# Attention probabilities through device memory: four block writes and one read in place of one write and four block reads

## The chip, the cores and the metric

One core of one Trainium2 chip runs the whole kernel in one launch. The metric is the device time of the execution in microseconds (us). A core has five engines that run side by side: TensorE (PE: matmuls; its weight loads are the row PEld), VectorE (DVE), ScalarE (ACT), GpSimd (POOL) and SyncE (SP), which here issues all transfers. Sixteen DMA engines move the bytes between device memory and the on-chip memory of 128 partitions.

## The reference

Two layers over 8 batches of 112 rows and 1024 columns, with 375 context rows per batch. Each layer adds a cross attention and then a small mixture of low-rank experts. The part that matters here is the second layer's attention, with 32 query heads over 8 key and value heads of width 128:

```python
q = (query @ wq).reshape(bs, sq, HQ, DK).transpose(0, 2, 1, 3)
k = (key @ wk).reshape(bs, sk, HKV, DK)
v = (value @ wv).reshape(bs, sk, HKV, DV)
...
q = apply_rope(q, pos)
k = apply_rope(k, curr_seq_pos + jnp.arange(sk))
scores = jnp.einsum('bhqd,bhkd->bhqk', q, k) / scale
...
attn = jax.nn.softmax(scores + m[:, None, :, :], axis=-1)
out = jnp.einsum('bhqk,bhkd->bhqd', attn, v)
out = out.transpose(0, 2, 1, 3).reshape(bs, sq, HQ * DV)
return out @ wo
```

## The kernel before, in words

Every large product is made of three float32r passes, from a high and a low part of each operand (`split_product`, L200): ScalarE makes the high part, GpSimd or VectorE the low one.

The second layer's attention runs in 64 steps, one for each of 8 groups (a key and value head with its four query heads) and 8 batches. All 64 steps are unrolled, in `attention_phase`. In step s TensorE makes the scores of step s+3, then adds a part of the output projection for an earlier quad of batches (`project`, two tiles of 448 columns, which needs weights of `wo`), then the product of probabilities and values of step s. VectorE masks scores, normalises and turns the probabilities of step s+2 and makes low parts; ScalarE takes the exponentials and makes high parts. ScalarE ends a step with `split_wo`, which waits for the next pieces of `wo` (names `e_raw_wo` and `e_wo_*`, L1902), and begins the next one with `take_output` (L1907), the high part of the last head output (`e_o_t_*`), whose low part VectorE then makes (L1977). `project` needs both parts.

For that product the probabilities must lie with the keys on the partitions. VectorE's transpose works within squares of 32 by 32 (L1739). The 112 queries are laid out as 4 blocks of 28 in a field of 4 blocks of 32 rows, and so the transpose leaves each key block j in the partitions of query block i. The blocks then have to change places, from (i; j) to (j; i), and this is done through device memory: `carry_out` writes the turned tile (`in_blocks`, shown as `q_rotated_then_x_rows`) to the internal tensor `probabilities`, and `carry_in` reads it back into `pt_raw` (two buffers, shown as `e_shuffled` and `e_shuffled_then_xn_t`). A tile is 128 partitions by 1536 float32, 768 KB.

SyncE carries out its instructions in order, one list for all transfers. In a step it does: `carry_out` of step s+2 (waits for the transpose), `load_qk` of step s+6, `load_v` of step s+2, `carry_in` of step s+2 (waits until the write has landed), then one or two pieces of `wo` (256 KB each; none in some steps). The order is written out by hand. All these transfers go through the same queue.

Of the kernel before, what the change touches and what calls it, by code (L numbers as in the profile page):

```python
# [12 lines left out]
F32 = mybir.dt.float32  # L13
# [5 lines left out]
P = 128  # L19
BATCH, SEQ, DIM = 8, 112, 1024  # L20
KEYS = 375
KEYS_EVEN = 376
KEY_TILES = 3
# [5 lines left out]
GROUPS, PER_GROUP = 8, 4  # L29
# [176 lines left out]
def build(nc, x, ctx_nat, ctx_t, mask, wq0_t, wk0, bq, bk, a0, b0, wq1, wk1, wv1, wo1, a1, b1,  # L206
          rope_q, rope_k, ident_in, tri0_in, order1_in, out):
    kt_dram = nc.dram_tensor("k_rotated", (BATCH, GROUPS, P, KEYS_EVEN), F32, kind="Internal").ap()
    v_dram = nc.dram_tensor("v_rows", (GROUPS, BATCH, P, KEY_TILES, P), F32, kind="Internal").ap()
    q_dram = nc.dram_tensor("q_rotated", (HEADS // 2, BATCH, P, 2, SEQ), F32, kind="Internal").ap()  # L210
    p_dram = nc.dram_tensor("probabilities", (2, P, BLOCKS, PER_GROUP * KEY_TILES * BLOCK), F32, kind="Internal").ap()
    x2_dram = nc.dram_tensor("x_after_layer0", (BATCH, SEQ, DIM), F32, kind="Internal").ap()
    with ExitStack() as outer:
        def sb(name, shape, dt=F32, ctx=outer):
            return ctx.enter_context(nc.sbuf_tensor(name, shape, dt))

        def sem(name, ctx=outer):
            return ctx.enter_context(nc.semaphore(name))

        banks = [outer.enter_context(nc.psum_tensor(f"bank{i}", [P, 512], F32)) for i in range(8)]  # L220
        k = Shared()
        k.x, k.ctx_nat, k.ctx_t, k.mask, k.ident_in, k.out = x, ctx_nat, ctx_t, mask, ident_in, out
        k.wq0_t, k.wk0, k.bq, k.bk = wq0_t, wk0, bq, bk
        k.wq1, k.wk1, k.wv1, k.wo1 = wq1, wk1, wv1, wo1
        k.a0, k.b0, k.a1, k.b1, k.tri0, k.order1 = a0, b0, a1, b1, tri0_in, order1_in
        k.rope_q, k.rope_k = rope_q, rope_k
        k.kt_dram, k.v_dram, k.q_dram, k.x2_dram, k.p_dram = kt_dram, v_dram, q_dram, x2_dram, p_dram
        k.banks, k.passed, k.sem = banks, sem("passed"), sem

        k.tables = sem("tables_in")  # L230
        k.ident, k.minus_half = sb("ident", [P, P]), sb("minus_half", [SEQ, 1])
        with ExitStack() as heads, ExitStack() as layer0:

            k.qp = sb("qp_then_xn3", [P, CH, TOK], ctx=layer0)
            k.qb = sb("q_dot_bk", [SEQ, BATCH], ctx=layer0)
            share_operands(nc, k, layer0)
            query_phase(nc, k)
            with ExitStack() as context, nc.Block() as block:

                keep, keep_pair, _ = buffers_of(nc, context)  # L240
                k.w_rest = keep_pair("w_rest", [P, CH - 2, DIM])
                keys, chunks = KeySems(sem), ContextSems(sem)
                k.layer0_only, k.k_stored = context, keys.stored
                q1 = QuerySems(sem)
                key_phase(nc, k, keys, chunks, block)
                layer0_phase(nc, k, keys, chunks, q1, heads, block)
                context.close()
                first = AttentionSteps(nc, heads, k)
                rotation = rotation_buffers(nc, layer0)
                layer0.close()  # L250
                late = attention_buffers(nc, heads, k, first)
                last_heads = query1_phase(nc, k, first, q1, rotation, block)
                attention_phase(nc, k, first, late, last_heads, heads, block)
# [1332 lines left out]
class AttentionSteps:  # L1586
# [140 lines left out]
    def transpose(self, dve, s, u, heads):  # L1727


        t, h = u % 2, heads[0]  # L1730
        if h == 0:
            dve.wait_ge(self.normed, 2 * s + 2)
            if s >= 2:
                dve.wait_ge(self.shuffled[t], 64 * (s // 2))
        else:
            dve.wait_ge(self.last_normed, 2 * s + 2)
        take_waits(dve, self.k.passed)
        piece = KEY_TILES * BLOCK
        dve.transpose(self.in_blocks[:, t, :, h * piece:(h + 2) * piece].rearrange("p j (m k) -> p m j k", k=BLOCK),  # L1739
                      self.s_buf[:, t, h:h + 2, :].rearrange("p h (c j k) -> p (h c) j k", j=BLOCKS, k=BLOCK)  # L1740
                      ).then_inc(self.transposed, 1)

    def carry_out(self, sp, s):


        t = s % 2
        sp.wait_ge(self.transposed, 2 * s + 2)
        if s >= 2:
            sp.wait_ge(self.shuffled[t], 64 * (s // 2))
        sp.dma_start(self.k.p_dram[t], self.in_blocks[:, t]).then_inc(self.carried, 16)  # L1750

    def carry_in(self, sp, s):


        t = s % 2
        sp.wait_ge(self.carried, 16 * s + 16)
        if s >= 2:
            sp.wait_ge(self.pt_low_first, s - 1)
            sp.wait_ge(self.pt_low, 2 * s - 2)
        for j in range(BLOCKS):  # L1760
            sp.dma_start(self.pt_raw[t][BLOCK * j:BLOCK * (j + 1)],  # L1761
                         self.k.p_dram[t, :, j].rearrange("(i a) x -> a i x", i=BLOCKS)).then_inc(
                self.shuffled[t], 16)

    def load_mask(self, sp):
        sp.dma_start(self.mask, self.k.mask).then_inc(self.mask_in, 16)
# [49 lines left out]
def attention_phase(nc, k, first, late, last_heads, ctx, block):  # L1816
# [79 lines left out]
    @block.scalar  # L1896
    def _(act):
        def split_wo(g, n):
            act.wait_ge(wo_in[n % 2], 16 * (4 * g + n // 2) + 16)
            if g > 0:  # L1900
                act.wait_ge(y_acc, 16 * g + n - 7)
            act.activation(wo_half(0, n), raw_wo[:, n % 2, 0], ACT.Copy).then_inc(wo_high, 1)  # L1902

        def take_output(s):
            u = s % BATCH
            act.wait_ge(o_acc, s + 1)
            act.activation(o_columns(ot[0][u // 4], u), by_block(o_banks[s % 2][:, 0:HALF]),  # L1907
                           ACT.Copy).then_inc(o_high, 1)

        def step(s, u, g):  # L1910
            if s >= 1:
                take_output(s - 1)
            if 0 < s < STEPS - 2:
                first.normalise_last(act, s + 2, u)
            act.wait_ge(first.shuffled[s % 2], 64 * (s // 2) + 64)
            for c in range(KEY_TILES):
                act.activation(by_block(pt[0][:, c, :]), raw_p(s, c), ACT.Copy).then_inc(pt_high, 1)  # L1917
            if s == 0:
                first.normalise_last(act, 2, u)
            if s + AHEAD < STEPS:  # L1920
                first.exps(act, s + AHEAD, u + AHEAD, (0, 1))
            if s + 5 < STEPS:
                first.qk_high_part(act, s + 5, u + 5)
            if s + AHEAD < STEPS:
                first.exps(act, s + AHEAD, u + AHEAD, (2, 3))
            if s + 1 < STEPS:
                first.v_high_part(act, s + 1, u + 1)
            for n in wo_splits(u, g):
                split_wo(g, n)

        steps(act, step)
        take_output(STEPS - 1)

# [197 lines left out]
def final_phase(nc, k, first, sem, block, y_added, y_of_quad):  # L2131
# [39 lines left out]
    @block.sync  # L2171
    def _(sp):
        sp.wait_ge(first.masked, 4 * GROUPS * BATCH)
        sp.wait_ge(first.qk_low, 2 * GROUPS * BATCH)
        sp.dma_start(aw[:, :, :], k.a1).then_inc(consts, 16)
        sp.dma_start(order, k.order1).then_inc(consts, 16)
        sp.dma_start(bw[:, :], k.b1).then_inc(consts, 16)

        def load(b):
            if b >= SLOTS:  # L2180
                sp.wait_ge(moved[b % SLOTS], 32 * (b // SLOTS))
            sp.dma_start(xr[:, b % SLOTS], k.x2_dram[b]).then_inc(moved[b % SLOTS], 16)

        for b in range(SLOTS):
            if b == 2:
                for s in first.shuffled:
                    sp.wait_ge(s, 64 * GROUPS * BATCH // 2)
            load(b)
        for b in range(LAST):
            sp.wait_ge(sl.added, 2 * b + 2)  # L2190
            sp.dma_start(k.out[b], xr[:, b % SLOTS]).then_inc(moved[b % SLOTS], 16)
            if b + SLOTS < BATCH:
                load(b + SLOTS)
        for h in range(2):
            cols = slice(h * 512, (h + 1) * 512)
            sp.wait_ge(sl.added, 2 * LAST + h + 1)
            sp.dma_start(k.out[LAST, :, cols], xr[:, LAST % SLOTS, cols]).then_inc(moved[LAST % SLOTS], 16)
        for i, s in enumerate(moved):
            sp.wait_ge(s, 32 * len(range(i, BATCH, SLOTS)) + (16 if i == LAST % SLOTS else 0))
# [232 lines left out]
```

## Time and profile before

| | |
|---|---|
| median of 3 runs | 1772.06 us (1770.04 to 1773.93) |
| profiled execution | 1774.46 us, of which the span from first to last instruction is 1772.7 us |
| TensorE, share of the span busy | 98% |
| VectorE, ScalarE, GpSimd | 62%, 41%, 44% |
| memory read and written | 193.01 MB and 97.26 MB, 164 GB/s over the span |
| write of a tile, and one of its four reads, from issue to landing | 4.7 us and 3.9 us in the median |

The profile shows one execution. Shares are of the whole span, which has stages with different limits; the attention of the second layer takes the part from about 1085 us to 1700 us. A row `SPq` is an instruction of SyncE's queue, where the time is that of issuing the transfer, and a row `DMA` is the transfer in flight.

### The profile page before, as it was taken

The page shows a single profiled execution, that of the slowest core. Times are in us where ns is not written, and L with a number is a line of the kernel's source. Part 1 is how long each engine was busy: PE and PEld are TensorE (multiplying, and loading weights), DVE is VectorE, ACT ScalarE, POOL GpSimd, SP SyncE. Part 2 cuts the span into 40 slices and gives each one's busy share as a digit, 9 for nine tenths or more (in the row PEclk, how much of TensorE's full clock was granted, in tenths as well). Part 3 has the DMA queues.
Part 4 walks back from the last instruction along what each step waited for, and adds up shares of the span by engine and source line. Part 5 has one row for each costly group of instructions (what it writes and reads, how often), then busy time and mean ns, then how long its engine had stood idle before and what let it go on. Part 6 is the DMA issues. An engine that isn't in the chain of part 4 may idle for free.

```text
span 1772.7 us, 26431 instructions
## 1 busy us (share of the span) xinstructions
PE 1736.4 (98%) x8904; PEld 1579.1 (89%) x8904; DVE 1101.1 (62%) x2116; ACT 733.5 (41%) x1532; POOL 782.3 (44%) x588
## 2 busy tenths in 40 slices
PE   6999999999999999999999999999999999999998
PEld 6999999999888888888999999889999899999986
DVE  7631276566433333336666668898888888888845
ACT  5211210012333232222101014477887888888724
POOL 3223522125422222201222234487787877877634
PEclk9999999999999999999999999999999999999999
DMA  4212442235643333423433335699999999999833
GB/s 140 63 49 83 133 133 84 85 104 162 208 128 119 111 116 118 128 82 95 129 109 91 106 113 163 200 291 272 274 277 274 270 275 281 276 272 281 257 117 111
DMA packets 186403, 291.55 MB, mean 164 GB/s; under 512 B 48337, under 2 KB 146897, under 8 KB 185281
## 3 DMA queue, kind: packets, MB, share of 16 engines
q1 hardware_dynamic: 186304, 290.33, 55.7%
q8 instruction: 51, 0.84, 0.2%
q14 instruction: 48, 0.39, 0.1%
HBM read 193.01 MB, written 97.26 MB: 164 GB/s over the span
## 4 chain that ended last, share of the span: by engine, by line
PE 70%; DMA 8%; DVE 5%; POOL 2%; issue 2%; ACT 2%; SPq 1%; DVEq 0%; ACTq 0%; POOLq 0%
PE bank L200 65%; DMA probabilities<-q_rotated_then_x_rows 3%; DMA e_raw_wo<-in_wo 3%; SPq L1761 1%; DVE e_scores L1696 1%; POOL shared_operand_low L324 1%; PE bank L106 1%; DVE q_rotated_then_x_rows L1739 1%; PE bank L2317 1%; DVE e_p_t_low L1982 1%; PE bank L186 1%; PE bank L2330 1%; DMA aw_weights_then_ctx_rows<-in_wv 1%; DMA aw_weights_then_ctx_rows<-in_wk 0%; DMA ctx_raw<-in_ctx_t 0%
## 5 line engine op out<-in xcount | busy, mean ns | idle before, releaser
L200 PE MATMUL bank<-shared_operand_high,w_first_high 128*128 128x448 f32 (+1 forms) x768 | 279.1, 363 | 1.9 <-DVE shared_operand_low L558 1.2
L200 PE MATMUL bank<-shared_operand_high,w_first_low 128*128 128x448 f32 (+1 forms) x768 | 278.4, 362 | 0.0
L200 PE MATMUL bank<-shared_operand_low,w_first_high 128*128 128x448 f32 (+1 forms) x768 | 278.3, 362 | 0.0
L324 POOL TENSOR_TENSOR shared_operand_low<-ctx_raw,shared_operand_high 128x768 fp32r<-128x768 f32 x64 | 119.2, 1875 | 199.6 <-ACT shared_operand_high L320 199.4
L1704 ACT ACTIVATE e_scores<-e_scores,e_least 128x375 f32<-128x375 f32 x256 | 153.5, 601 | 44.9 <-DVE e_least L1696 44.9
L1452 POOL TENSOR_TENSOR w_first_low<-aw_weights_then_ctx_rows,w_first_high 128x1024 fp32r<-128x1024 f32 x30 | 72.2, 2407 | 221.1 <-ACT w_first_high L1420 221.1
L200 PEld LDWEIGHTS bank<-shared_operand_high,w_first_high 128*128 128x128 f32 x768 | 144.7, 188 | 13.1 <-POOL w_first_low L496 1.4
L200 PEld LDWEIGHTS bank<-shared_operand_low,w_first_high 128*128 128x128 f32 x768 | 144.8, 189 | 11.0
L200 PEld LDWEIGHTS bank<-shared_operand_high,w_first_low 128*128 128x128 f32 x768 | 144.6, 188 | 11.0
L320 ACT ACTIVATE shared_operand_high<-ctx_raw 128x768 fp32r<-128x768 f32 x64 | 52.8, 843 | 211.8 <-DMA ctx_raw<-in_ctx_t 193.2
L1696 DVE CUSTOM_DVE_ANT_0 e_scores<-bank,e_mask_then_layer_ffn 128x375 f32<-128x375 f32 x256 | 134.8, 529 | 0.0
L1420 ACT ACTIVATE w_first_high<-aw_weights_then_ctx_rows 128x1024 fp32r<-128x1024 f32 x30 | 31.8, 1060 | 236.7 <-PE bank L200 194.8
L200 PE MATMUL bank<-shared_operand_high,w_rest_high 128*128 128x376 f32 x384 | 128.7, 335 | 0.2 <-POOL w_rest_low L789 0.2
L200 PE MATMUL bank<-shared_operand_high,w_rest_low 128*128 128x376 f32 x384 | 128.6, 335 | 0.0
L200 PE MATMUL bank<-shared_operand_low,w_rest_high 128*128 128x376 f32 x384 | 128.6, 335 | 0.0
L1739 DVE STREAM_TRANSPOSE q_rotated_then_x_rows<-e_scores 128x768 f32<-128x768 f32 x128 | 124.1, 970 | 0.3 <-DVE e_scores L1717 0.3
L200 PE MATMUL bank<-w_rest_high,shared_operand_high 128*128 128x512 f32 x288 | 112.9, 392 | 0.0
L200 PE MATMUL bank<-w_rest_high,shared_operand_low 128*128 128x512 f32 x288 | 112.4, 390 | 0.0
L200 PE MATMUL bank<-w_rest_low,shared_operand_high 128*128 128x512 f32 x288 | 112.3, 390 | 0.0
L1939 POOL TENSOR_TENSOR e_p_t_low<-e_shuffled_then_xn_t,e_p_t_high 128x448 fp32r<-128x448 f32 x64 | 84.0, 1333 | 40.7 <-ACT e_p_t_high L1917 40.6
L1939 POOL TENSOR_TENSOR e_p_t_low<-e_shuffled,e_p_t_high 128x448 fp32r<-128x448 f32 x64 | 83.9, 1332 | 35.6 <-ACT e_p_t_high L1917 35.5
L1025 ACT ACTIVATE v_out<-bank 128x512 f32<-128x512 f32 x48 | 28.6, 596 | 171.3 <-PE bank L200 171.3
(259 smaller groups left out, 4614.7 us busy)
## 6 DMA issues: line engine op xcount, KB each, us to landing
probabilities<-q_rotated_then_x_rows SPq DMA_DIRECT2D x64, 768.0 KB, 4.7
ctx_raw<-in_ctx_t SPq DMA_DIRECT2D x64, 384.0 KB, 3.9
e_shuffled_then_xn_t<-probabilities SPq DMA_DIRECT2D x128, 192.0 KB, 3.9
e_shuffled<-probabilities SPq DMA_DIRECT2D x128, 192.0 KB, 3.9
e_raw_wo<-in_wo SPq DMA_DIRECT2D x64, 256.0 KB, 4.8
aw_weights_then_ctx_rows<-in_wq SPq DMA_DIRECT2D x30, 512.0 KB, 4.0
q_rotated<-q_rotated_then_x_rows SPq DMA_DIRECT2D x64, 224.0 KB, 2.3
e_raw_then_a<-q_rotated SPq DMA_DIRECT2D x64, 224.0 KB, 5.0
```

Source lines behind the costliest of these rows:

```text
L106: last = pe.transpose(banks[j][:, c * SEQ:(c + 1) * SEQ], buf.xn[:, k, ch * P:(ch + 1) * P], ident[0:SEQ, 0:SEQ])
L186: last = pe.matmul(mid[:, 0:width], xnt[:, c, :], aw[:, c, :], start=(c == 0), stop=(c == CH - 1))
L200: mm = pe.matmul(out, stationary[a], moving[b], start=(first and i == 0), stop=(last and i == 2))
L320: act.activation(k.ctx_ring[0][slot][:, 2 * j:2 * j + 2, :], k.c_raw[:, j % 2], ACT.Copy).then_inc(done, 1)
L324: pool.tensor_tensor(k.ctx_ring[1][slot][:, 2 * j:2 * j + 2, :], k.c_raw[:, j % 2], f32(k.ctx_ring[0][slot][:, 2 * j:2 * j + 2, :]), ALU.s ...
L1025: act.activation(v_out[:, p % 2], v_bank[p % 2][:, :], ACT.Copy).then_inc(v_read, 1)
L1420: act.activation(k.w_first[0][:, t], k.raw[:, t], ACT.Copy).then_inc(w_high, 1)
L1452: pool.tensor_tensor(k.w_first[1][:, t], k.raw[:, t], f32(k.w_first[0][:, t]), ALU.subtract).then_inc(w_low, 1)
L1696: dve.tensor_tensor_reduce(self.s_buf[:, t, h, 0:KEYS], self.s_bank[h][:, 0:KEYS], self.mask[:, u, :], 1.0, HIGHEST, ALU.add, ALU.min, sel ...
L1704: act.activation(self.s_buf[:, t, h, 0:KEYS], self.s_buf[:, t, h, 0:KEYS], ACT.Exp, bias=self.least[:, t, h:h + 1], scale=-1.0, accum_out= ...
L1739: dve.transpose(self.in_blocks[:, t, :, h * piece:(h + 2) * piece].rearrange("p j (m k) -> p m j k", k=BLOCK), self.s_buf[:, t, h:h + 2, : ...
L1939: pool.tensor_tensor(by_block(pt[1][:, c, :]), raw_p(s, c), by_block(f32(pt[0][:, c, :])), ALU.subtract).then_inc(pt_low, 1)
```

## The change

The internal tensor is laid out by destination instead of by source: its second index is the key block j, the third the row within the block, the fourth the query block i. The write is now four transfers, one for each query block i, each from 32 partitions with four pieces of 1536 bytes to where they belong. The read is one transfer of 128 rows of 6144 bytes. The counts that others wait for follow: a write now adds 64 to its semaphore, a read 16. Lines behind the functions move up by one.

```diff
-    p_dram = nc.dram_tensor("probabilities", (2, P, BLOCKS, PER_GROUP * KEY_TILES * BLOCK), F32, kind="Internal").ap()
+    p_dram = nc.dram_tensor("probabilities", (2, BLOCKS, BLOCK, BLOCKS, PER_GROUP * KEY_TILES * BLOCK), F32, kind="Internal").ap()
...
-                dve.wait_ge(self.shuffled[t], 64 * (s // 2))
+                dve.wait_ge(self.shuffled[t], 16 * (s // 2))
...
         if s >= 2:
-            sp.wait_ge(self.shuffled[t], 64 * (s // 2))
-        sp.dma_start(self.k.p_dram[t], self.in_blocks[:, t]).then_inc(self.carried, 16)
+            sp.wait_ge(self.shuffled[t], 16 * (s // 2))
+        for i in range(BLOCKS):
+            sp.dma_start(self.k.p_dram[t, :, :, i].rearrange("j a x -> a j x"),
+                         self.in_blocks[BLOCK * i:BLOCK * (i + 1), t]).then_inc(self.carried, 16)
...
-        sp.wait_ge(self.carried, 16 * s + 16)
+        sp.wait_ge(self.carried, 64 * s + 64)
...
-        for j in range(BLOCKS):
-            sp.dma_start(self.pt_raw[t][BLOCK * j:BLOCK * (j + 1)],
-                         self.k.p_dram[t, :, j].rearrange("(i a) x -> a i x", i=BLOCKS)).then_inc(
-                self.shuffled[t], 16)
+        sp.dma_start(self.pt_raw[t], self.k.p_dram[t].rearrange("j a i x -> (j a) i x")).then_inc(self.shuffled[t], 16)
...
-            act.wait_ge(first.shuffled[s % 2], 64 * (s // 2) + 64)
+            act.wait_ge(first.shuffled[s % 2], 16 * (s // 2) + 16)
```

On SyncE, in the kernel before, the first steps of the attention stand like this (a row with x4 is four transfers, one after the other):

```order
L1750 DMA probabilities<-q_rotated_then_x_rows 128x1536
L1632 DMA e_raw_then_a<-q_rotated 128x2x224
L1634 DMA e_raw_then_a<-k_rotated 128x376
L1639 DMA e_raw_then_a<-v_rows 128x384
L1761 DMA e_shuffled_then_xn_t<-probabilities 32x4x384 x4
L1875 DMA e_raw_wo<-in_wo 128x512
```

The changed kernel has the same place with the four in front:

```order
L1751 DMA probabilities<-q_rotated_then_x_rows 32x4x384 x4
L1632 DMA e_raw_then_a<-q_rotated 128x2x224
L1634 DMA e_raw_then_a<-k_rotated 128x376
L1639 DMA e_raw_then_a<-v_rows 128x384
L1762 DMA e_shuffled_then_xn_t<-probabilities 128x1536
L1874 DMA e_raw_wo<-in_wo 128x512
```

The loads of q, k and v now stand behind four transfers instead of one, and the load of `wo` behind one instead of four; nothing changes its place otherwise.

## Rows read from the trace of the kernel before

**Rows 1.** The page's busy row, and busy time by stage with its columns
```profile
PE 1736.4 (98%) x8904; PEld 1579.1 (89%) x8904; DVE 1101.1 (62%) x2116; ACT 733.5 (41%) x1532; POOL 782.3 (44%) x588
...
core 0: us, PE busy (x) PEld busy (x) DVE busy (x) ACT busy (x) POOL busy (x), PEclk, DMA share, GB/s
...
1240.00:1684.00 444.00, 439.06 (x2234) 411.24 (x2234) 377.27 (x840) 358.20 (x886) 345.37 (x295) 1.00 0.95 274
```

**Rows 2.** TensorE's waits, 1240 to 1700 us: total us, times, longest
```profile
PE bank L200 <- DVE e_o_t_first_low L1977: 4.9, 5, 2.0
PE bank L200 <- DVE e_o_t_second_low L1977: 2.2, 1, 2.2
```

**Rows 3.** The chain that ended last, 1369 to 1384 us: start, us, what
```profile
1369.65 5.15 DMA probabilities<-q_rotated_then_x_rows
...
1374.81 0.33 SPq L1761
...
1376.13 0.43 SPq L1761
...
1377.08 5.13 DMA e_raw_wo<-in_wo
...
1382.23 0.63 ACT e_wo_third_high L1902
1382.86 0.44 ACT e_o_t_first_high L1907
...
1383.33 0.64 DVE e_o_t_first_low L1977
```

**Rows 4.** Busy time by stretch behind two stalls, columns as in rows 1
```profile
1384.00:1388.00 4.00, 4.00 (x12) 3.58 (x13) 4.00 (x10) 4.00 (x11) 3.52 (x4) 0.57 0.88 215
1388.00:1392.00 4.00, 4.00 (x22) 3.70 (x21) 2.39 (x7) 2.09 (x6) 3.36 (x4) 1.00 1.04 314
1694.00:1698.00 4.00, 3.71 (x11) 3.36 (x12) 1.20 (x2) 0.67 (x2) 2.68 (x3) 0.60 1.04 309
```

**Rows 5.** The whole chain that ended last, share of the span by line
```profile
by line: PE bank L200 65.5%; DMA probabilities<-q_rotated_then_x_rows 3.2%; DMA e_raw_wo<-in_wo 2.7%; issue 1.9%; SPq L1761 1.1%; DVE e_scores L1696 1.0%; POOL shared_operand_low L324 0.9%; PE bank L106 0.8%; DVE q_rotated_then_x_rows L1739
```

**Rows 6.** All 64 writes, L1750: issue in ns, first and last; landing
```profile
L1750 SPq DMA_DIRECT2D probabilities<-q_rotated_then_x_rows x64: 326/338/504, 1087.9 to 1681.2; - x64
...
DMA to landing us min/median/max: 3.8/4.7/6.7
```

**Rows 7.** SyncE's queue in the last step: start, us of issue, what
```profile
1685.96 1.74 SPq L1761 DMA_DIRECT2D e_shuffled<-probabilities  x4
1687.75 0.43 SPq L1875 DMA_DIRECT2D e_raw_wo<-in_wo  x1
```

**Rows 8.** SyncE's own waits before the reads: total us, times, longest
```profile
SPq L1761 <- DMA probabilities<-q_rotated_then_x_rows: 131.4, 64, 4.0
```

**Rows 9.** Landing of the four reads issued from 1685.96 us
```profile
DMA to landing us min/median/max: 3.0/3.8/4.3
```

**Rows 10.** Transfers by line: count, KB each, median us from issue to landing
```profile
k_rotated<-k_rotated_sb SPq DMA_DIRECT2D x64, 188.0 KB, 1.9
...
aw_weights_then_ctx_rows<-in_ctx_nat SPq DMA_DIRECT2D x7, 1536.0 KB, 6.6
aw_weights_then_ctx_rows<-in_wk SPq DMA_DIRECT2D x16, 512.0 KB, 3.6
```

**Rows 11.** ScalarE's timeline: the wait for wo behind those last reads
```profile
1692.21 0.63 ACT L1902 ACTIVATE e_wo_fourth_high<-e_raw_wo 128x512 fp32r<-128x512 f32 x1 [5.27 <-DMA e_raw_wo<-in_wo]
```

**Rows 12.** 448 KB over 112 partitions: seven stores, L2191, and three loads, L2182
```profile
DMA to landing us min/median/max: 3.1/3.1/3.5
...
DMA to landing us min/median/max: 3.4/3.5/3.5
```

**Rows 13.** Two stores of 224 KB, L1354, issued one behind the other
```profile
L1354 SPq DMA_DIRECT2D q_rotated<-q_rotated_then_x_rows x2: 434/474/513, 1118.1 to 1118.6; - x2
...
DMA to landing us min/median/max: 6.1/6.2/6.3
```

More of the change, by code:

```diff
@@ L2186, in _ @@
                 for s in first.shuffled:
-                    sp.wait_ge(s, 64 * GROUPS * BATCH // 2)
+                    sp.wait_ge(s, 16 * GROUPS * BATCH // 2)
             load(b)
```

## The prediction

> **What bounds the kernel now.** I read the stages first [rows 1]. TensorE is busy for 1736 of 1773 us. In the long middle stage (1240 to 1684) TensorE is busy for 439.1 of 444 us, and the 16 DMA engines for 0.95 of the time: both are nearly full, at full clock. The transfers that change lie behind 1087 us; the change can gain only what TensorE loses from there on.
>
> That loss is in the waits of the matmuls [rows 2]: 4.9 us in five waits and 2.2 us in one, together 7.1 us, all for a split head output (DVE, L1977). The chain shows why that comes late [rows 3]: last transpose of the probabilities, the write of them (5.15 us), four issues of reads on SyncE's queue, two loads of wo (the second in flight 5.13 us), the split of that weight on ScalarE, and only behind it ScalarE's copy of the head output, then DVE's, then TensorE, which had been idle for 2 us. ScalarE stands in line for wo, and wo stands in SyncE's queue behind the probabilities. The kernel pays for a stall a second time: after the one at 1384 us and the one at 1694 us the granted clock is 0.57 and 0.60 over the next 4 us, a mean between the levels of 1.2 and 2.4 GHz, against 1.00 afterwards; 12 matmuls run in 4 us where 22 do then, so that each stall costs some 1.6 us more [rows 4].
>
> How often does this chain set the end? Of the whole chain, 3.2% are these writes, 2.7% loads of wo and 1.1% issues of the four reads [rows 5]. 1.1% of 1772.7 is 19.5 us; a set of four takes 1.75 us (from 1374.81 to the end of the one of 1376.13, [rows 3]), so 11 passes of the 64.
>
> **The change, part by part.** Per step it removes one write of 128 rows and four reads of 32 partitions, and adds four writes of 32 partitions and one read of 128 rows. Bytes, number of transfers and waits of other engines stay.
>
> *Issue on SyncE.* One plain write costs 0.34 us [rows 6], four reads 1.74 [rows 7]. The other way about, the four writes take about 1.8 and the read 0.34. The write side gets 1.4 us longer, and the loads of q, k and v behind it leave 1.4 us later. They have cover: SyncE afterwards waits for the write, 131.4 us in 64 times, 2.05 us a step [rows 8], and these loads are for steps 6 and 2 ahead. Without that cover a late v would hold ScalarE by the same 1.4 us. The read side gets 1.4 us shorter, and wo leaves that much earlier.
>
> *The read.* The last four reads show what pieces cost. The first lands 3.0 us after its issue, the last 4.3 us after its own [rows 9], which begins 1.3 us after the first (1374.81 and 1376.13 in [rows 3]), so the set needs 5.6 us. Three pieces in 5.6 - 3.0 = 2.6 us is 0.87 us for 192 KB. A whole read of 768 KB isn't in the trace. From loads over all 128 partitions, 512 KB in 3.6 and 1536 KB in 6.6 [rows 10], 768 KB interpolate to 3.6 + 3.0/4 = 4.35, say 4.4 us. So here the read would land 1.2 us sooner than the set. Bounds: nothing, if memory and not the pieces sets the pace, and 1.9 us (5.6 less the 3.8 of the fastest whole write, [rows 6], rounded up). I take 1.2, near the interpolated value.
>
> Does wo's earlier issue bring anything by itself? In the last step wo is issued at 1687.75 [rows 7], 0.5 after the fourth read (1687.3), which lands at 1691.6 with its 4.3 us. ScalarE begins on wo at 1692.21 [rows 11], so wo lands no more than 0.6 us behind the reads. It flows behind the reads' data in the same queues, so it lands when they have drained, not 1.4 us sooner. I count 0.1 for it.
>
> *The write.* A whole write lands in 3.8 at best, 4.7 in the median, 6.7 at worst [rows 6]. Written in pieces of 32 partitions: one small store over 128 partitions lands in 1.9 (188 KB) [rows 10]; a piece of 32 partitions needs 0.3 more if stores suffer as loads do (0.87 us for 192 KB in pieces, 0.56 at the 3.0 us for 1024 KB of the whole loads), then three more at 0.87 to 1.0 each: 1.9 + 0.3 + 2.8 = 5.0 us on free queues, against 3.8 for the whole one at best [rows 6]. That is 1.2 us later. Do stores suffer like loads? The nearest rows: a store of 448 KB over 112 partitions lands in 3.1 us and the load of the same shape in 3.4 to 3.5 [rows 12], so one shape costs nearly the same in both directions. Bounds: nothing (then the writes are done when the last, issued 1.4 us late, lands 1.9 later, 3.3 us, inside the present 4.7), and 1.9 us, the mirror of the read's.
>
> The Trainium skill (SBUF — State Buffer, Door 1: The DMA port swizzle) says that 32 partitions reach 8 of the 16 ports, with 189 GB/s measured at 1 MiB against 328 for all 128. By that estimate 768 KB would take 1.8 us longer in pieces, so the write would lose 1.8 and the read win 1.8, and the sum would be the same. The trace's pieces, 0.87 us for 192 KB, are 226 GB/s, nearer to the rule's slow figure than to its fast one. The same skill (DMA: Bandwidth & Descriptors, Rules for kernel authors) advises one transfer over 128 partitions in place of several over parts; it speaks against the write's half of the change and for the read's.
>
> *The sum.* Per pass: read -1.2, wo -0.1, write +1.2: -0.1 us. Over 11 passes about -1 us, which lies within the 7.1 us of waits that could be saved. The profiled execution took 1774.46 us, 1772.70 of them span, so it would take 1773.4; it lies 2.4 us above the median of 1772.06. From the median: **1771.0 us**.
>
> **The rivals.**
> *A: stores don't suffer.* TensorE would gain 1.2 or 1.3 us a pass. The stalls are at most 2.2 us long and a stall often follows on two passes, so most of the 7.1 us go and with them up to 3.2 us of low clock: 6 to 10 us, 1762 to 1766, say 1764.5. For it speaks that small stores over 128 partitions land in 1.9 us; against it the like times of load and store in [rows 12]. Chance 0.25.
> *B: the write gets longer by more than the read gets shorter.* The place is SyncE's wait before the read. It decides as soon as the last of the four writes lands more than 1.3 us later than the whole write does (6.0 in the median). At the bound of 1.9 a pass costs 0.6 us, 11 passes 6.6 us, and 5 to 8 us if a stall more or less falls to the low clock: 1778.5. For it: the DMA engines are at 0.95, so nothing absorbs a longer transfer, and where pieces of two kinds overlap (a slow read of wo behind, writes ahead) both may slow. Against: the read's gain has the same cause as the write's loss. Chance 0.22.
> *C: each write waits for its predecessor to be confirmed in memory.* The trace has two stores of 224 KB issued 0.5 us apart, which land 6.1 and 6.3 us after their issues, that is 0.7 us apart [rows 13]: back to back. With a full small-store latency of 1.9 each, the four would take 7.6, 2.9 later than now, or 1.6 a pass after the gain of 1.3: 11 times 1.6 is 18 us, 1790. Chance 0.03.
> The Trainium skill (DMA: Bandwidth & Descriptors, Anatomy of one DMA) states that the semaphore fires only when the last byte is confirmed, slowest when memory is the target; this is the only reading under which C would follow, and the two stores speak against it.
>
> **How the numbers follow.** Within 0.2% (3.5 us) is about what a measurement here can tell from no change. The forecast, read and write cancel to within 0.4 us a pass, has 0.50 and its own range is 1768 to 1775. A 0.25, B 0.22, C 0.03. The range takes in the middle of A and of B: 1764.5 to 1778.5; beyond it lie C, the far half of A and part of B, 2 in 10. Faster by over 0.2%: A and a little of the forecast, 0.29. Slower: B, C and a sliver, 0.26. Same: 0.45.
>
> **What the changed profile would show.** The issues on SyncE's queue: four writes with about 0.45 us each, one read with 0.34. Landing of the writes: the last should land 5.5 to 6.2 us after the first one's issue (rival A: 4.7 or less, B: over 6.2). Landing of the read: 4.2 to 4.8 (median), against 5.6 to 6 for the set before. Landing of the pair: 10.4 to 10.8 us after the last transpose in both kernels. The waits of TensorE for L1977 should stay between 5 and 8 us, and at most two stretches with a low clock. Share of the DMA engines 0.93 to 0.97 in the middle stage. My prediction is wrong if the whole read lands no sooner than the set did, or if the loads of k and v, pushed back by 1.4 us, start to hold ScalarE: a row of waits for e_v_high or e_k_high beyond 2 us would show it.

## The result, and the profile after

The changed kernel takes 1797.88 us in the median of 4 runs (1794.87 to 1801.64), the kernel before 1772.74 us in the median of 4 runs of the same session. The ratio is 1.0146 with a 95% interval from 1.0129 to 1.0164: slower by 25 us, where 1771.0 was predicted and 1778.5 was the upper end of the range. That is 1.5%, and the interval lies clear of 1. The profiled execution of the changed kernel took 1798.12 us.

The page's busy row and the middle stage of the changed kernel, with the columns of [rows 1]:

```profile
PE 1747.0 (97%) x8904; PEld 1583.3 (88%) x8904; DVE 1103.5 (61%) x2116; ACT 733.3 (41%) x1532; POOL 783.1 (44%) x588
...
1240.00:1684.00 444.00, 426.62 (x2144) 395.50 (x2143) 365.02 (x811) 345.75 (x859) 336.26 (x287) 0.99 0.87 265
```

TensorE does the same 8904 matmuls in 10.6 us more busy time (1747.0 against 1736.4), and outside them the span has 49.3 us instead of 36.3 (1796.3 - 1747.0 and 1772.7 - 1736.4). These two, 10.6 and 13.0, are the whole difference of the spans, 23.6 us. The 13.0 are idle time. Of the 10.6 only a part is the price of the clock. Spans and mean granted clock, first of the kernel before, then of the changed one:

```profile
core 0: 1772.7 us, clock 0.997
core 0: 1796.3 us, clock 0.995
```

A share of 0.003 of 1772.7 us is 5 us of full-speed work that is missing, 0.005 of 1796.3 us is 9, so the clock explains some 4 of the 10.6 us. Another 2.2 stand ahead of 1080 us, where both kernels are alike (1064.0 us busy in the one trace, 1066.3 in the other). What the last 4 us are was not taken apart. Four microseconds at a time (same columns; the third from the end is the granted clock) the trace shows how they hang together:

```profile
1392.00:1396.00 4.00, 1.56 (x9) 1.24 (x8) 0.27 (x2) 1.77 (x4) 1.14 (x2) 1.00 0.99 337
1396.00:1400.00 4.00, 3.37 (x11) 3.05 (x12) 4.00 (x11) 4.00 (x11) 3.46 (x4) 0.70 0.68 222
1400.00:1404.00 4.00, 4.00 (x19) 3.65 (x19) 2.54 (x8) 2.60 (x7) 4.00 (x5) 0.87 0.78 215
1404.00:1408.00 4.00, 4.00 (x23) 3.85 (x22) 3.30 (x9) 2.82 (x6) 1.15 (x2) 1.00 0.93 255
```

TensorE stands idle for 2.4 of 4 us, and in the next two stretches, at a granted clock of 0.70 and 0.87, it does 11 and 19 matmuls where 23 go at full clock, as in [rows 4]. The DMA engines are less busy than before, 0.87 against 0.95: the change relieves them and still loses time. (Over the same stretch the share is 0.84 in the kernel below with the single read alone and 0.95 in the one with the four writes alone, so the relief is the single read's.)

TensorE's waits from 1240 to 1700 us (total us, times, longest), to be read beside [rows 2]:

```profile
PE bank L200 <- DVE e_o_t_first_low L1976: 9.8, 7, 3.1
PE bank L200 <- DVE e_p_t_low L1981: 7.2, 5, 2.3
PE bank L200 <- DVE e_o_t_second_low L1976: 0.6, 1, 0.6
```

Together 17.6 us instead of 7.1, and with a second kind: the low part of the next probabilities (L1981) is late too, because VectorE itself is: in this stretch it waits 64.6 us for ScalarE's high parts of the output, where it waited 57.3 in the kernel before. The whole chain by line, to be read beside [rows 5]:

```profile
by line: PE bank L200 53.1%; DMA e_raw_wo<-in_wo 7.4%; DMA probabilities<-q_rotated_then_x_rows 5.2%; issue 3.6%; DVE e_scores L1696 2.2%; DVE q_rotated_then_x_rows L1739 1.8%; DVE e_p_t_low L1981 1.6%; SPq L1751 1.4%; DVE e_scores L1717 1.
```

Counted piece by piece from 1080 us on, the chain passes over a load of wo 21 times, and 10 times in the kernel before, in 64 steps. The stretch of the chain that corresponds to [rows 3] (start, us, what):

```profile
1368.78 6.69 DMA e_raw_wo<-in_wo
...
1375.49 0.63 ACT e_wo_first_high L1901
1376.12 0.44 ACT e_o_t_first_high L1906
...
1376.59 0.07 DVE e_o_t_first_low L1976
...
1379.28 0.93 DVE e_p_t_low L1981
...
1380.67 0.90 DVE q_rotated_then_x_rows L1739
...
1381.59 0.33 SPq L1751
...
1382.92 3.79 DMA probabilities<-q_rotated_then_x_rows
...
1386.73 0.33 SPq L1762
...
1387.58 7.26 DMA e_raw_wo<-in_wo
...
1395.95 0.64 DVE e_o_t_first_low L1976
1396.63 9.55 PE bank L200 x39
```

This is the row that the prediction had not looked for. Between 1375.49 and 1381.59 the chain does not go through TensorE at all: from the landing of wo it goes over ScalarE and VectorE to the next transpose, and from there into the next write. It closes into a loop: transpose, write, read, wo, ScalarE, VectorE, transpose. One turn takes two steps: these loads of wo follow the read of one step, and the transpose that they hold back belongs to the step after the next. The part from the landing of wo to the next write is 6.1 us (1375.47 to 1381.59), the part from the write's first issue to the landing of wo 13.25 us (1381.59 to 1394.84).

The transfers by line on the page (KB each, median us from issue to landing; before, the write took 4.7 and one of the four reads 3.9):

```profile
probabilities<-q_rotated_then_x_rows SPq DMA_DIRECT2D x256, 192.0 KB, 3.6
...
e_shuffled_then_xn_t<-probabilities SPq DMA_DIRECT2D x32, 768.0 KB, 5.5
e_shuffled<-probabilities SPq DMA_DIRECT2D x32, 768.0 KB, 5.7
e_raw_wo<-in_wo SPq DMA_DIRECT2D x64, 256.0 KB, 5.8
```

The single read takes 5.5 to 5.7 us, where 4.2 to 4.8 was predicted. SyncE's queue shows what stands ahead of it. First one step of the kernel before, then one of the changed kernel (start, us of issue, what):

```profile
1369.65 0.34 SPq L1750 DMA_DIRECT2D probabilities<-q_rotated_then_x_rows  x1
1370.03 0.43 SPq L1632 DMA_DIRECT2D e_raw_then_a<-q_rotated  x1
1370.51 0.97 SPq L1634 DMA_DIRECT2D e_raw_then_a<-k_rotated  x1
1371.52 1.19 SPq L1639 DMA_DIRECT2D e_raw_then_a<-v_rows  x1
1374.81 1.75 SPq L1761 DMA_DIRECT2D e_shuffled_then_xn_t<-probabilities  x4
```

```profile
1381.59 2.29 SPq L1751 DMA_DIRECT2D probabilities<-q_rotated_then_x_rows  x4
1383.93 0.79 SPq L1632 DMA_DIRECT2D e_raw_then_a<-q_rotated  x1
1384.76 0.92 SPq L1634 DMA_DIRECT2D e_raw_then_a<-k_rotated  x1
1385.73 0.45 SPq L1639 DMA_DIRECT2D e_raw_then_a<-v_rows  x1
1386.73 0.33 SPq L1762 DMA_DIRECT2D e_shuffled_then_xn_t<-probabilities  x1
```

Before, the issue of v ends 2.1 us ahead of the reads (1372.71 and 1374.81); now 0.55 us ahead of the read (1386.18 and 1386.73), so that more of their data is still to come. Over the steps 13 to 60 v lands 1.6 us after the reads' first issue in the kernel before and 2.5 us after the read's issue in the changed one (medians).

### The profile page after: what moved, and what is told of

Same layout as the page of the kernel before. It is cut to its first block, busy times and chain, and to the rows that moved or that the text cites. A ratio compares the mean times of both kernels' runs of the same rounds, so it can differ in the third digit from the quotient of the medians.

```text
span 1796.3 us, 26431 instructions
## 1 busy us (share of the span) xinstructions
PE 1747.0 (97%) x8904; PEld 1583.3 (88%) x8904; DVE 1103.5 (61%) x2116; ACT 733.3 (41%) x1532; POOL 783.1 (44%) x588
## 4 chain that ended last, share of the span: by engine, by line
PE 57%; DMA 14%; DVE 9%; issue 4%; ACT 2%; SPq 2%; POOL 1%; DVEq 0%; ACTq 0%; POOLq 0%
PE bank L200 53%; DMA e_raw_wo<-in_wo 7%; DMA probabilities<-q_rotated_then_x_rows 5%; DVE e_scores L1696 2%; DVE q_rotated_then_x_rows L1739 2%; DVE e_p_t_low L1981 2%; SPq L1751 1%; DVE e_scores L1717 1%; PE bank L106 1%; PE bank L2316 1%; PE bank L186 1%; PE bank L2329 1%; POOL shared_operand_low L324 1%; DMA aw_weights_then_ctx_rows<-in_wk 0%; DVE y_t L1970 0%
## 5 line engine op out<-in xcount | busy, mean ns | idle before, releaser
L1717 DVE TENSOR_SCALAR e_scores<-e_scores,e_inv 128x375 f32<-128x375 f32 x128 | 99.0, 775 | 2.2
```

What stands on the lines that cost most here:

```text
L1717: dve.tensor_scalar(self.s_buf[:, t, h, 0:KEYS], self.s_buf[:, t, h, 0:KEYS], self.inv[:, t, h:h + 1], None, ALU.mult).then_inc(self.norme ...
```

## The experiments

The main readings of all kernels stand in one table. For each of the steps 13 to 60 the trace gives the end of the last transpose (T), the issue of each transfer and its landing; the figures are medians over these 48 steps, in us. "Write" and "read" are from the first issue of the set to its last landing, "T to T" is from one T to the next. Wo is loaded in 42 of these 48 steps; in the two kernels with a dash it is not behind the read. The time is the median, the ratio is to the kernel before in the same session, with its 95% interval.

| kernel | write | read | T to reads landed | T to wo landed | T to T | time, ratio |
|---|---|---|---|---|---|---|
| before | 4.72 | 6.01 | 10.98 | 11.61 | 8.76 | 1772.74 |
| changed | 5.42 | 5.81 | 11.62 | 12.40 | 9.23 | 1797.88, 1.0146 |
| w4_r4 | 5.70 | 6.30 | 12.16 | 12.94 | 9.33 | 1805.27, 1.0182 (1.0165 to 1.0199) |
| w1_r1_noswap | 4.06 | 4.34 | 8.48 | 9.50 | 8.76 | 1763.54, 0.9952 (0.9936 to 0.9969) |
| w4rows_r4 | 5.53 | 6.36 | 12.04 | 12.83 | 9.43 | 1807.28, 1.0201 (1.0184 to 1.0218) |
| w4spread_r1 | 5.20 | 5.35 | 10.83 | 11.69 | 8.79 | 1783.98, 1.0061 (1.0045 to 1.0077) |
| w1short_r4 | 4.80 | 5.96 | 11.07 | 11.74 | 8.86 | 1774.47, 1.0016 (1.0001 to 1.0030) |
| before_qkv_first | 6.39 | 5.79 | 13.99 | 14.86 | 10.46 | 1858.14, 1.0503 (1.0482 to 1.0524) |
| after_qkv_first | 7.68 | 4.35 | 13.26 | 14.52 | 10.14 | 1844.03, 1.0403 (1.0381 to 1.0426) |
| before_qkv_last | 4.70 | 5.95 | 10.58 | 11.38 | 10.35 | 1859.34, 1.0490 (1.0465 to 1.0514) |
| after_qkv_last | 5.46 | 4.32 | 9.93 | 11.02 | 9.98 | 1858.28, 1.0478 (1.0460 to 1.0497) |
| before_wo_first | 4.23 | 6.31 | 10.96 | - | 8.76 | 1763.09, 0.9955 (0.9939 to 0.9972) |
| after_wo_first | 5.75 | 6.36 | 12.22 | - | 8.76 | 1765.51, 0.9955 (0.9937 to 0.9972) |

**The write half alone.** Four writes, and four reads, whose rows now lie whole in device memory (6144 bytes, where they were gathered from pieces of 1536):

```diff
-        sp.dma_start(self.k.p_dram[t], self.in_blocks[:, t]).then_inc(self.carried, 16)
+        for i in range(BLOCKS):
+            sp.dma_start(self.k.p_dram[t, :, :, i].rearrange("j a x -> a j x"),
+                         self.in_blocks[BLOCK * i:BLOCK * (i + 1), t]).then_inc(self.carried, 16)
...
+            sp.dma_start(self.pt_raw[t][BLOCK * j:BLOCK * (j + 1)], self.k.p_dram[t, j]).then_inc(self.shuffled[t], 16)
```

> The write's half of the change alone: four scattered writes from 32 partitions each, and four reads into 32 partitions each. Before takes 1772.7, the changed kernel 1797.9. If the loss lies in the writes and in the loads of q, k and v that they push back, and the whole read gives something back, this is the slowest: 1803 to 1815, writes landing 5.4 in the median (4.7 before), set of reads 6.0 to 6.7. Rival, the loss lies in the whole read (it stands undivided behind other loads): 1772 to 1780 here.

It is 1.82% slower, 32 us, and so worse than the whole change. The writes land 1.0 us later, and T to wo grows by 1.3 us. The four reads gain nothing from their whole rows (6.30 against 6.01), so it is not the run length that makes a single read quicker.

**The read half alone.** One write, one read, the exchange left out:

```diff
-        for j in range(BLOCKS):
-            sp.dma_start(self.pt_raw[t][BLOCK * j:BLOCK * (j + 1)],
-                         self.k.p_dram[t, :, j].rearrange("(i a) x -> a i x", i=BLOCKS)).then_inc(
-                self.shuffled[t], 16)
+        sp.dma_start(self.pt_raw[t], self.k.p_dram[t]).then_inc(self.shuffled[t], 16)
```

> The read's half alone: one write and one read of 128 rows each; the exchange of the blocks is left out, so the probabilities reach the product in the wrong places. If the whole read is as quick as the best rows say (4.4 us free), it lands 4.8 to 5.2 in the median against 6.0 for the set before, and the kernel takes 1762 to 1768. Rival, a whole read brings nothing in this stream of transfers: lands 5.6 or more, time within 2 us of 1772.7.

Here the read lands 1.7 us sooner (4.34 against 6.01), more than the 1.2 of the prediction, and T to wo falls by 2.1 us. V lands 1.6 us after the read's issue, as before, so the loads ahead of it have the same lead. The write, which is the one of before, lands 0.7 us sooner too (4.06 against 4.72). The time falls by only 9 us. TensorE's waits from 1240 to 1700 us and the busy time of that stretch say why there is no more to win:

```profile
PE bank L200 <- DVE e_o_t_second_low L1974: 0.4, 1, 0.4
PE bank L2314 <- ACT e_shuffled_then_xn_t L2203: 0.3, 1, 0.3
PE bank L200 <- issue: 0.2, 1, 0.2
...
1240.00:1700.00 460.00, 459.03 (x2357) 430.45 (x2356) 381.14 (x860) 362.97 (x896) 355.26 (x302) 1.00 0.83 274
```

The two halves apart give +32 us (1.82%) and -8.5 us (0.48%), together some +24, near the +25 of the change. The cost of the writes has no such end, while the read's gain ends with the stalls that were there. But the sum does not show that the halves are independent: the single read lands in 4.34 us here and in 5.81 behind four writes.

**Why four writes of 32 partitions take longer.** Three kernels take apart the number of partitions and the length of the runs. First, four writes of 32 partitions with each row in one run of 6144 bytes, and four reads as before:

```diff
+        for i in range(BLOCKS):
+            sp.dma_start(self.k.p_dram[t, BLOCK * i:BLOCK * (i + 1)],
+                         self.in_blocks[BLOCK * i:BLOCK * (i + 1), t]).then_inc(self.carried, 16)
```

> The kernel before with its one write cut into four of 32 partitions, each with rows of 6144 bytes in one piece of memory. Theory P (32 partitions reach only half of the ports into the on-chip memory): the last write lands 5.0 on free queues and 5.4 to 6 in the median, time 1800 to 1815, as with the scattered writes. Theory R (runs of 1536 bytes scattered in memory are what is slow): it lands 3.8 at best and 4.7 in the median, time 1772 to 1780.

As slow as the pieces of 1536 bytes: the write takes 5.53 us against 5.70, the time is 1807.28 against 1805.27. Then the other way round, one write of 128 partitions in runs of 1536 bytes:

```diff
-        sp.dma_start(self.k.p_dram[t], self.in_blocks[:, t]).then_inc(self.carried, 16)
+        sp.dma_start(self.k.p_dram[t].rearrange("j p x -> p j x"), self.in_blocks[:, t]).then_inc(self.carried, 16)
```

> The kernel before with its one write of 128 partitions laid out by key block, so that it goes out in runs of 1536 bytes that lie 192 KB apart, and four reads that find each piece in one block of 192 KB. Theory P: nothing is lost, write lands 3.8 at best and 4.7 in the median, 1770 to 1776. Theory R: the write gets as slow as four scattered ones (5.0 at best), 1785 to 1800.

4.80 us against 4.72, and a ratio of 1.0016: short runs cost next to nothing. Last, the changed kernel with each write taken from every fourth partition:

```diff
-                         self.in_blocks[BLOCK * i:BLOCK * (i + 1), t]).then_inc(self.carried, 16)
+                         self.in_blocks[i::BLOCKS, t]).then_inc(self.carried, 16)
```

> The changed kernel with each of its four writes taken from every fourth partition instead of 32 neighbouring ones, destinations and counts unchanged; the rows land in wrong places, so the exchange is not done rightly. Theory P: all ports are reached, the last write lands 3.9 to 4.4 on free queues instead of 5.0 and the kernel comes back to 1770 to 1782. Theory R, or the mere number of transfers and their late followers: as the changed kernel, 1793 to 1802, landing 5.0 at best.

The rows of the writes, first of the changed kernel, then of this one (issue in ns, min, median, max; landing of a single write in us):

```profile
L1751 SPq DMA_DIRECT2D probabilities<-q_rotated_then_x_rows x256: 318/442/1582, 1089.0 to 1706.4; - x128
...
DMA to landing us min/median/max: 2.3/3.6/7.6
```

```profile
L1751 SPq DMA_DIRECT2D probabilities<-q_rotated_then_x_rows x256: 577/606/1890, 1085.9 to 1682.8; - x128
...
DMA to landing us min/median/max: 2.3/2.8/5.1
```

The same bytes in the same number of writes land in 2.8 us each instead of 3.6, though the issue of each takes 0.16 us more. Of the steps 13 to 60 the best set lands 4.25 us after its first issue, where 5.0 is the best of the changed kernel and 4.04 of the whole write. In the median the set gains less, 5.20 against 5.42. The time is 1783.98 us, 13.9 less than the changed kernel's, and 2 us outside the range that was expected. Its 8 runs go from 1770.83 to 1786.40 us, and the trace is of the fastest, 13 us below the median. So its row of the table, T to T above all, tells of an execution that lost nothing against the kernel before, and not of the median one, which loses 11 us. The neighbouring partitions thus account for something over half of the time that the change costs, and for three quarters of what the best set loses, but for only 0.2 of 0.7 us in the median set. The rest would lie in the number of writes and the longer issues, which no run took apart; run length has next to no part. The Trainium skill (SBUF — State Buffer, Door 1: The DMA port swizzle) states that 32 consecutive partitions reach 8 of the 16 ports; by the same table every fourth partition reaches all 16. The runs agree in direction, and for stores: 5.0 and 4.25 us for the best sets.

**What the read waits for.** The theory now was that the single read gains little because q, k and v lie ahead of it in the queue, 1.8 us later than they used to (the issue of v ends 4.63 us after T instead of 2.82). In this kernel their four lines are moved up, ahead of the writes:

```diff
+            if s + 6 < STEPS:
+                first.load_qk(sp, s + 6, (u + 6) % 8, g + (u + 6) // 8)
+            if s + 2 < STEPS:
+                first.load_v(sp, s + 2, (u + 2) % 8, g + (u + 2) // 8)
             if s + 2 < STEPS:
                 first.carry_out(sp, s + 2)
```

> The changed kernel with the loads of q, k and v issued ahead of the four writes (in the time that SyncE waits for the transpose) instead of behind them. Theory Q (these loads, pushed back, lie ahead of the whole read): the read lands 4.5 to 5.0 in the median instead of 5.8, the way from the last transpose to wo gets 0.7 us or more shorter (12.4 now), and the kernel takes 1775 to 1785. Rival, the DMA engines are simply full: the same bytes in another order, 1793 to 1802.

> The same exchange of order in the kernel before. Theory Q: the reads begin as soon as the write has landed, the set lands 5.4 instead of 6.0, 1764 to 1770. Rival, engines full: 1772 to 1776.

The times were a miss in both: the loads had no idle time ahead of the transpose to hide in, pushed the write back, and it then lay behind them (7.68 and 6.39 us). But the read landed in 4.35 us after the whole load had gone ahead, and the set of four in 5.79, hardly sooner than in the old order (5.4 was expected). The other order moves q, k and v down, behind the read and wo:

```diff
             if s + 2 < STEPS:
                 first.carry_in(sp, s + 2)
             for of, n in wo_loads(u, g):
                 load_wo(of, n)
+            if s + 6 < STEPS:
+                first.load_qk(sp, s + 6, (u + 6) % 8, g + (u + 6) // 8)
+            if s + 2 < STEPS:
+                first.load_v(sp, s + 2, (u + 2) % 8, g + (u + 2) // 8)
```

> The changed kernel, with q, k and v loads issued behind the read and the pieces of wo instead of between write and read. By theory Q (the single read lands no earlier than the four did because it stands behind q, k and v loads that the four writes had made late) the read now lands in 4.3 to 4.8 us from its issue, and the wo pieces 11.2 to 11.6 us after the transpose instead of 12.4: 1768 to 1785 us. The v loads issue some 10 us later than now, which is still five steps' work ahead only for q and k, not for v; if v then holds TensorE or ScalarE the time rises over 1800 us and only the landing of the read counts as a test. If the read takes 5.4 us or more even so, Q is wrong and the single read is itself no faster behind the four writes.

> The kernel before with the same order as after_qkv_last: write, wait, four reads, wo, then q, k and v. By Q the four reads are bound by themselves, not by the loads ahead, and land in 5.4 to 6.0 us from the first issue; so the single read gains 0.8 us or more beside after_qkv_last where it gained 0.2 us in the order as it was. If both kernels' reads land alike here too, the single read has no gain to give in this kernel. Time 1760 to 1790 us, with the same risk of a late v.

Both kernels are slow by the late loads, as the expectation feared for v, but it is q that holds ScalarE. ScalarE's waits of the changed kernel in this order, 1240 to 1700 us:

```profile
ACT e_q_high L1646 <- DMA e_raw_then_a<-q_rotated: 134.3, 44, 6.2
ACT e_k_high L1649 <- DMA e_raw_then_a<-k_rotated: 5.9, 11, 1.0
```

So only the landings test the theory, and they bear it out, although both of these orders also lengthen the step to some 10 us and so spread the same transfers over more time. All reads of one line, first the single read in this order, then the single read of the changed kernel, us from issue to landing:

```profile
DMA to landing us min/median/max: 4.1/4.3/5.6
```

```profile
DMA to landing us min/median/max: 4.3/5.6/7.7
```

The trace of the changed kernel shows the same by itself, at its own pace. In 24 of the steps 13 to 60 the read is issued less than 0.7 us after the issue of v has ended, and lands in 6.3 us in the median; in the 16 steps with at least 1.4 us in between it lands in 4.5.

With nothing fresh ahead the single read gains 1.6 us on the set of four (4.32 against 5.95), and T to wo comes out 0.4 us shorter than with the kernel before in this order (11.02 against 11.38), although the writes are 0.8 us longer. That is the balance which the prediction had expected of the change itself.

**Why it costs 25 us and not 9.** The loads of wo are issued ahead of the wait for the write, from step 8 on; in the kernel before, and then in the changed one:

```diff
             if s + 2 < STEPS:
                 first.load_v(sp, s + 2, (u + 2) % 8, g + (u + 2) // 8)
...
+            if s >= 8:
+                for of, n in wo_loads(u, g):
+                    load_wo(of, n)
             if s + 2 < STEPS:
                 first.carry_in(sp, s + 2)
-            for of, n in wo_loads(u, g):
-                load_wo(of, n)
+            if s < 8:
+                for of, n in wo_loads(u, g):
+                    load_wo(of, n)
```

> The kernel before with the pieces of wo (from the second group on) issued ahead of SyncE's wait for the write instead of behind the reads. Theory L (the loop from transpose over write, reads and wo to ScalarE and back to the transpose two steps later is what stalls TensorE): wo no longer waits for the exchange, TensorE's waits for L1977 between 1240 and 1700 us fall from 7.1 to under 2 us, 1762 to 1767. Rival, wo is only the last of several that are late (probabilities, v): 1770 to 1775 with the waits moved to L1982.

> The changed kernel, with the pieces of wo issued ahead of the wait that carry_in begins with, from step 8 on, as in before_wo_first. By theory L (the loop from the transpose over the write, the read, the wo pieces and ScalarE has no slack, so that what the write adds is paid at nearly every second step) the pieces of wo leave the chain, ScalarE's waits for them go, and most of the 25 us that the change cost comes back: TensorE's waits for VectorE's L1976 between 1240 and 1700 us fall from 9.8 to under 3 us, 1764 to 1776 us. If the loss came from the higher load on the queue itself (rival), the wo pieces issued between write and read make the read later still and the time stays above 1785 us.

TensorE's waits from 1240 to 1700 us and the busy time of that stretch, of the changed kernel in this order:

```profile
PE bank L200 <- DVE e_o_t_first_low L1980: 0.6, 1, 0.6
PE bank L200 <- DVE e_o_t_second_low L1980: 0.4, 1, 0.4
...
1240.00:1700.00 460.00, 459.01 (x2350) 430.77 (x2349) 386.98 (x865) 369.71 (x909) 361.38 (x309) 1.00 0.92 279
```

In the kernel before, the same edit leaves one wait of 0.4 us. All of the loss is gone, though the read now takes 6.36 us and T to reads landed is the longest of the kernels with a step of 8.76 us, 12.22. Both orders of the probabilities come out at a ratio of 0.9955, the medians at 1763.09 and 1765.51: with wo out of the loop the change costs nothing that can be measured. Either of them beats both original kernels.

## Why the prediction was wrong

Two steps of the prediction failed, the read's "-1.2" and "over 11 passes". Through the first a pass came out 0.8 us longer instead of 0.1 shorter. Over 11 passes that is 9 us, an estimate of some 1781 us, which lies beyond the range already. The second is the way from those 9 us to the 25.

- **The read, "-1.2".** The term was -0.2 us in the median (6.01 to 5.81; -0.5 in the mean, 6.12 to 5.65). Alone the read gains more than predicted, 1.7 us in the read half alone, 1.4 and 1.6 in the pairs with q, k and v elsewhere. The interpolated 4.4 us was right for a read with no fresh load just ahead of it (4.3). What failed is the step before it, on issue: "the loads of q, k and v behind it leave 1.4 us later. They have cover". They left 1.8 us later. They do not hold ScalarE in earnest (from 1240 to 1700 us 7 waits for q, 5.1 us together, and 0.4 us for k; two waits for v behind 1700 us, 1.7 us together), but they use up the pause in which most of their data had drained ahead of the read. A cover was counted for the engines that use the loads and not for the transfer queued behind them. With wo ahead of the read as well its gain was nothing (6.31 and 6.36).
- **What bounds the kernel, and the number of passes.** The chain was read rightly for the kernel before: 11 passes from the shares, 10 or 11 by count. The step that failed is the multiplication "over 11 passes", which took that number as fixed. From the landing of wo to the next write's issue the chain takes 6.1 us; with 11.61 us from T to wo that makes 17.7, with 12.40 it makes 18.5. Two steps of TensorE without a stall are 17.5 us (twice 8.76). The loop had no slack in the kernel before (it was 0.2 us over) and is 1.0 us too long in the changed one, and half of 18.5 is 9.25 us, where the trace has 9.23 from T to T. For w4_r4 and w4rows_r4 the same sum gives 9.5, where the table has 9.33 and 9.43. A loss therefore counts in most turns of the loop (21 passes in 32 pairs of steps), while a gain ends as soon as the 7.1 us of waits and their low clock are gone. The experiments with wo ahead of the wait show that this loop, and no other way from the transfers to TensorE, costs the time.
- **The write, "+1.2".** The mechanism was right in good part and the size nearly so: +0.7 us in the median (4.72 to 5.42) and +1.1 in the mean (4.83 to 5.90), +1.0 in the write half alone, in good part by the partitions that each write reaches. Stores suffer too; rival A falls.
- **wo, "-0.1".** It was +0.15: wo now lands 0.8 us behind the reads in the difference of the medians (12.40 - 11.62), 0.6 before (11.61 - 10.98).
- **Sum of a pass.** 0.8 us longer (11.61 to 12.40) in place of 0.1 shorter. Rival B had named the place, SyncE's wait before the read, but priced it by 11 passes, at 1778.5. With the measured 0.8 us those 11 would give 9 us, and 21 give 17. That 17 is an estimate; with the 4 us of the clock it comes to some 21, where the spans differ by 23.6.
- **Rival C** would have put the writes' last landing at 7.6 us; it is 5.42.
- **What the profile was to show.** Issue of a write 0.44 us (predicted 0.45) and of the read 0.33 (0.34): right. Last landing of the writes 5.42, just under 5.5 to 6.2. T to reads landed 11.6, outside 10.4 to 10.8, and in the kernel before 10.98, outside as well. Landing of the read 5.8, outside 4.2 to 4.8. Waits for the head output 10.4 us, outside 5 to 8. Stretches of low clock behind 1085 us: four, where at most two were forecast. DMA share 0.87, outside 0.93 to 0.97, through the single read, as the 0.84 and 0.95 of the two halves show. Neither of the two signs that were to prove it wrong came out clearly: the read did land 0.2 us sooner, and no wait for k or v passed 2 us. The loss came by a way that they did not cover, the loads ahead of the read.

## What to carry to other kernels

Count the slack of the loop before counting passes: add up one turn of the chain, over all engines and transfers, and set it beside the time that the busiest engine needs for the same steps. If they are equal, a loss counts at every turn and a gain hardly at all, and the cheapest repair is to take the member that needs nothing of the exchange (here the loads of wo, behind a wait that was not theirs) out of the queue order. And a transfer that is issued later costs whoever is queued behind it, even where its own user has time.

## What the runs showed of the hardware

- At best of 48 steps a set of four writes of 192 KB from 32 neighbouring partitions each lands in 5.0 us, from every fourth partition in 4.25, and one write of 128 partitions in 4.04, each in one trace; runs of 1536 bytes instead of 6144 cost 0.08 us in the median.
- An issue on SyncE's queue is not of fixed length. Of the four writes one takes up to 1.58 us where 0.44 is the median, and the load of q behind them 0.76 us in the median where it took 0.43 behind a single write. What sets the length was not tested.
- Taking every fourth partition lengthens the issue itself, from 0.44 to 0.61 us in the median.
- A single read of 768 KB lands in 4.3 us where the loads of q, k and v (604 KB) are out of its way, and in 6.3 us in the steps where it is issued less than 0.7 us behind them.
